# Two of the three weighted one-hot multiplications of the edge preparation issued from GpSimd, and the item's registers loaded inside each step

## The chip, the cores and the metric

One core of a Trainium2 chip runs the whole kernel. The metric is the device time of one execution in microseconds (us). Before the change it is 13,212.99 us, the median of 3 runs.

## What is computed

Four graph layers one after another over 6,250 nodes with 128 features and 200,000 edges sorted by target node; each adds its result to the node features and normalises them.

```python
edge_index = jnp.stack([src, dst])
x = _layernorm(x + _L0_gnn_ref(x, edge_index, edge_weight, ...))       # GCN: segment_sum of h[src] * norm
x = _layernorm(x + _L1_gnn_ref(x, edge_index, edge_type_8, ...))       # gated graph network, 2 rounds, GRU
x = _layernorm(x + _L2_gnn_ref(x, edge_index, ...))                    # graph attention, 8 heads
x = _layernorm(x + _L3_gnn_ref(x, edge_index, edge_attr_64, ...))      # message passing with edge features
# in the GCN: deg = segment_sum(w, dst); norm = deg**-.5[src] * w * deg**-.5[dst]
```

The change lies in a stage that computes no layer by itself. It sorts the edges into records that the layers then read.

## The kernel before

The kernel runs in stages, each a block in which every engine has its own program, with semaphores between the engines. The stage `prep` (its buffers are named `prep_...`) comes third, after the setup of the weights and the making of the work list.

The edges are cut into groups of 1,792 (128 partitions x 14 columns, `GC = 14`). An item is one group seen against one tile of 128 target nodes, 112 items in all; items come from a list in memory, four in each turn of the loop (`SL = 4`), 28 turns. Buffers indexed by `par` are double, by the parity of the item.

For item k the engines do this:

- **SyncE** loads the item's four numbers (base node, column, group, record place) into `itm[:, s]`, two items ahead.
- **GpSimd** (`pool`, lines 687 to 706) loads the group's number into a register, waits until the item two before is through with its buffers, and copies what belongs to the group: L694 and L695 (target and key of each edge), after a wait L698 to L700 (differences to the item's bases), L701, L702 and L704 (the edge's fields: `fld`, two numbers; `w2`, the weight in three bf16 parts, each stored twice; `wm`). The last raises `posted`.
- **VectorE** (`dve`) runs, in one turn of its loop for item k, five functions: `key_hot(k)`, `rank_hot(k-1)`, `rec_add(k-2)`, `weigh_keys(k)`, `window_hot(k)`.
  - `key_hot`: L771 and L772 make the key, L776 the one-hot matrix `OJ` (14 x 98 columns, bf16), which raises `hot_key`; L778, L780 and L781 count equal keys ahead of each edge.
  - `rank_hot`: L795 and L796 take TensorE's counts out of PSUM, L799 and L801 make the rank, L802, L803 the one-hot of the rank, `OHr`; L806 keeps the rank in `RK`.
  - `rec_add`: L816 adds TensorE's placed records to `RECS`, L819 its sums of weights to `acc`.
  - `weigh_keys`: L828, three times: `OJF[..., 2 + a, :] = OJ * w2[a]`, raises `wdone`.
  - `window_hot`: L835 makes the one-hot of the target node, raises `hotd`.
- **ScalarE** scales `OJ` by the two numbers of `fld`: L720, 28 times per item, into `OJF[..., 0:2, :]`, raises `scaled`.
- **TensorE** runs `ranks(k)` (L909 to L914: counts by key), `place(k-1)` (L924: 14 products of `OHr` with all five parts of `OJF`, 490 columns) and `degrees(k)` (L933).

A chain (`Chain.step`, line 91) orders VectorE's dependent steps: each step raises the chain's semaphore at its end, and the engine waits for that count at once, before anything else:

```python
    def step(self, ins):
        ins.then_inc(self.sem, 1)
        self.n += 1
        self.eng.wait_ge(self.sem, self.base + self.n)
```

Addresses that depend on the item come from registers. `places(s)` (lines 784 to 788) increments a semaphore (`passed`) and loads three: the group `g`, the record place `b0` and the column `col`. VectorE calls it once per item ahead of `key_hot` (`now`), which in the order of the program is right behind `window_hot` of the item before, and once more at the start of each turn of the loop (`last`). `rank_hot` and `rec_add` are handed the registers. `w2` and the views `pairs` and `halves` serve the multiplications as pairs of bf16 values.

Of the kernel before, what the change touches and what calls it, by code (L numbers as in the profile page):

```python
# [30 lines left out]
ALU = mybir.AluOpType  # L31
# [80 lines left out]
def build(nc, x, src, dst, edge_attr_64, edge_type_8, edge_weight, L0_gnn_W, L0_gnn_b, L1_gnn_node_proj_w,  # L112
# [47 lines left out]
    with ExitStack() as whole:  # L160
# [442 lines left out]
        with ExitStack() as ctx:  # L603
# [41 lines left out]
            zeroed, posted, hotd, hot_key, scaled, wdone, prefix_ready, prefix_free, hot_rank, place_ready, place_free = sems(  # L645
                "prep", "zeroed posted hotd hot_key scaled wdone prefix_ready prefix_free hot_rank place_ready place_free")
# [5 lines left out]
            with nc.Block() as block:  # L652
# [26 lines left out]
                def _(pool):  # L679
                    pool.wait_ge(zeroed, 1)  # L680
                    n = pool.value_load(turns_to[0:1, NCH:NCH + 1], min_val=1, max_val=KCAP // SL)
                    with pool.Fori(0, n) as i:
                        for s in range(SL):
# [8 lines left out]
                            pool.wait_ge(hotd, k + 1)  # L692
                            fg = FLD[:, ds(g, 1)].rearrange("p g f c -> p (g f) c")
# [11 lines left out]
                            pool.wait_ge(posted, k + 1)  # L705
                            passed(pool, tick)

# [26 lines left out]
                def _(dve):  # L734
# [17 lines left out]
                    dve.sem_inc(scaled, 2)  # L752
                    dve.sem_inc(wdone, 2)
# [12 lines left out]
                    def key_hot(k, s, own):  # L766
# [7 lines left out]
                        dve.wait_ge(scaled, k + 1)  # L774
                        dve.wait_ge(wdone, k + 1)
# [8 lines left out]
                    def places(s):  # L784
                        passed(dve, tick)
                        return (dve.value_load(itm[0:1, s, 2:3], min_val=0, max_val=NG - 1),
                                dve.value_load(itm[0:1, s, 3:4], min_val=0, max_val=(NT - 2) * NT),
                                dve.value_load(itm[0:1, s, 1:2], min_val=0, max_val=N - 1))

                    def rank_hot(k, s, own, at_):  # L790
                        par = s % 2
                        n0 = own.n
                        g, b0, _ = at_
# [16 lines left out]
                    def rec_add(k, s, own, at_):  # L810
                        par = s % 2
                        n0 = own.n
                        _, b0, col = at_
                        dve.wait_ge(place_ready, k + 3)
                        rec = RECS[:, :, ds(b0, BK)]
                        own.step(V.tensor_tensor(out=rec, in0=rec, in1=placed[par].rearrange("p (f b) -> p f b", f=5), op=ALU.add))  # L816
                        dve.sem_inc(place_free, 1)
                        dve.wait_ge(product, k + 3)
                        own.step(V.tensor_tensor(out=acc[0:4, ds(col, P)], in0=acc[0:4, ds(col, P)], in1=dps[par], op=ALU.add))  # L819
                        dve.sem_inc(done, 1)  # L820
                        assert own.n - n0 == ADD_STEPS

                    def weigh_keys(k, s):
# [3 lines left out]
                        for a in range(3):  # L827
                            ins = V.tensor_tensor(out=halves(OJF[:, par, :, 2 + a, :]), in0=halves(OJ[:, par]),  # L828
                                                  in1=pairs(w2[:, par, a], BK), op=ALU.mult)
                        ins.then_inc(wdone, 1)  # L830
# [8 lines left out]
                    with dve.Fori(0, n) as i:  # L839
                        own = Chain(dve, chain)  # L840
                        own.base = i * (SL * STEPS)
                        last = places(SL - 2)
                        for s in range(SL):
                            k = i * SL + s
                            now = places((s - 1) % SL)
                            key_hot(k, s, own)
                            rank_hot(k - 1, (s - 1) % SL, own, now)
                            rec_add(k - 2, (s - 2) % SL, own, last)
                            last = now
# [6 lines left out]
                    last, now = places(SL - 2), places(SL - 1)  # L856
                    rank_hot(n * SL - 1, SL - 1, own, now)
                    rec_add(n * SL - 2, SL - 2, own, last)
                    rec_add(n * SL - 1, SL - 1, own, now)
# [40 lines left out]
                def _(pe):  # L900
# [16 lines left out]
                    def place(k, s):  # L917
                        par = s % 2
                        pe.wait_ge(hot_rank, k + 2)
                        pe.wait_ge(scaled, k + 3)  # L920
                        pe.wait_ge(wdone, k + 3)
# [1405 lines left out]
```

## Time and profile before

| | us |
|---|---|
| median of 3 runs | 13,212.99 |
| the runs | 13,180.84 to 13,275.48 |
| the profiled execution | 13,180.84 |
| its span in the profile | 13,178.7 |
| `prep` loop, first to last item's start | 1,382.6 |

The profile shows one execution. Engines are PE (TensorE matmul), PEld (its weight load), DVE (VectorE), ACT (ScalarE), POOL (GpSimd); a "q" behind a name is the engine's sequencer, whose register and semaphore instructions are not counted as busy. L828 is line 828 of the kernel. Over the whole span PE is busy 47%, DVE 42%, POOL 38%, ACT 12%; these are means over stages with different limits, so the stage's own windows are to be read. "Idle before" names what ended an idle time: another engine's instruction, or "issue" where the profile shows nothing that the engine waited for. The ends of matmuls are modelled.

### The profile page before, as it was taken

The numbers are of one execution on the slowest core, as the hardware profiler recorded it, in microseconds if no ns is written. First come the engines' busy times: TensorE is split into PE (matmuls) and PEld (weight loads), VectorE is DVE, ScalarE is ACT, GpSimd is POOL, SyncE is SP. The second block draws the span as 40 slices with busy tenths as digits, with TensorE's granted clock in tenths as the row PEclk, the third lists the DMA queues.
The fourth block names the chain that finished last, engine by engine and source line by source line (L and its number), as shares of the span: only waits on it lengthen the run. The fifth ranks groups of instructions, "written<-read, shape, count | busy, mean of one in ns | idle before, by whom it ended". The sixth has DMA issues, their size and how long they took to land. (4 is left out here: it accounts for less than half of the span.)

```text
span 13178.7 us, 173973 instructions
## 1 busy us (share of the span) xinstructions
PE 6156.4 (47%) x63984; PEld 5201.2 (39%) x63985; DVE 5472.2 (42%) x6618; ACT 1595.2 (12%) x4258; POOL 5038.6 (38%) x5706
## 2 busy tenths in 40 slices
PE   1666669963233332322222223666996233333344
PEld 1333369951222222212222223556996133333333
DVE  2888878852011111111101114997886312212223
ACT  0666620001000000000000000111000001111111
POOL 0111100002666666566665662000000365565564
PEclk6777789986565666656555555557997566666666
DMA  9000032232112221111111112553221121221121
GB/s 39 0 0 0 0 69 83 83 82 75 45 52 53 55 53 53 50 53 43 43 46 39 42 43 85 207 207 106 94 93 52 46 62 51 54 62 51 52 61 48
DMA packets 572278, 802.99 MB, mean 61 GB/s; under 512 B 400316, under 2 KB 444730, under 8 KB 552872
## 3 DMA queue, kind: packets, MB, share of 16 engines
q1 hardware_dynamic: 397096, 427.95, 12.4%
q0 software_dynamic: 153216, 312.49, 9.4%
q10 hardware_dynamic: 21888, 61.54, 1.2%
q8 instruction: 46, 0.75, 0.0%
q14 instruction: 32, 0.26, 0.0%
HBM read 719.59 MB, written 81.99 MB: 61 GB/s over the span
## 5 line engine op out<-in xcount | busy, mean ns | idle before, releaser
L1088 POOL DMA_INDIRECT ggnn_edges_G<-trans_d,ggnn_edges_idx x3136 | 3117.4, 994 | 2049.5 <-DMA ggnn_edges_idx<-row_d 1102.7
L1196 PE MATMUL ggnn_edges_PS<-ggnn_edges_OH,ggnn_edges_G 128*128 128x128 f32 x6272 | 1081.4, 325 | 2589.1 <-issue 1645.5
L1088 POOL DMA_INDIRECT mpnn_edges_G<-msg_d,mpnn_edges_idx x1568 | 1553.7, 991 | 1398.0 <-DMA mpnn_edges_idx<-src_d 919.1
L1196 PEld LDWEIGHTS ggnn_edges_PS<-ggnn_edges_OH,ggnn_edges_G 128*128 128x128 f32 x6272 | 989.2, 238 | 2687.6 <-issue 2685.8
L1149 DVE TENSOR_TENSOR acc<-acc,ggnn_edges_PS 128x128 f32 x224 | 64.5, 288 | 3034.7 <-remote 2509.9
L720 ACT ACTIVATE prep_OJF<-prep_OJ,prep_fld 128x98 bf16<-128x98 bf16 x3136 | 848.9, 362 | 577.8 <-DVE prep_OJ L776 577.8
L1196 PE MATMUL mpnn_edges_PS<-mpnn_edges_OH,mpnn_edges_G 128*128 128x128 f32 x3136 | 502.3, 307 | 401.1 <-issue 364.0
L924 PE MATMUL prep_PS<-prep_OJF,prep_OHr 128*128 128x490 bf16 x1582 | 582.2, 550 | 226.2 <-DVE prep_OHr L803 226.2
L1174 PE MATMUL mpnn_edges_PS<-wt_late,mpnn_edges_atT 64*128 64x128 f32 x3136 | 351.0, 340 | 667.4 <-ACT mpnn_edges_atT L1064 313.2
L1196 PEld LDWEIGHTS mpnn_edges_PS<-mpnn_edges_OH,mpnn_edges_G 128*128 128x128 f32 x3136 | 450.3, 218 | 456.7 <-issue 452.4
L1376 PE MATMUL heads_GP<-heads_hd,heads_msg 128*128 128x128 f32 x4900 | 590.3, 277 | 0.0
L1376 PE MATMUL gcn_GP<-gcn_hd,gcn_msg 128*128 128x128 f32 x4900 | 590.3, 277 | 0.0
L1174 PEld LDWEIGHTS mpnn_edges_PS<-wt_late,mpnn_edges_atT 64*128 64x128 f32 x3136 | 287.2, 237 | 724.5 <-issue 395.0
L1376 PEld LDWEIGHTS heads_GP<-heads_hd,heads_msg 128*128 128x128 f32 x4900 | 562.8, 192 | 0.1
L1376 PEld LDWEIGHTS gcn_GP<-gcn_hd,gcn_msg 128*128 128x128 f32 x4900 | 562.8, 192 | 0.0
L2027 PE MATMUL ba_XP<-ba_A,ba_hsT 128*128 128x16 bf16 x7350 | 408.4, 174 | 320.2 <-DVE ba_hdT L1911 318.2
L1113 DVE SCALAR_TENSOR_TENSOR ggnn_edges_OH<-dstI,ggnn_edges_itm,iota_row 128x1792 f32<-128x1792 f32 x224 | 464.6, 2084 | 191.7 <-issue 176.5
L1136 DVE TENSOR_TENSOR mpnn_edges_G<-mpnn_edges_G,mpnn_edges_PS 128x896 f32<-128x896 f32 x224 | 233.3, 1082 | 737.1 <-DMA trans_d<-ggnn_edges_tb 610.3
L1536 ACT ACTIVATE ggnn_edges_OH<-ggnn_edges_PS,bcol 128x896 f32<-128x896 f32 x14 | 14.1, 1007 | 4258.0 <-issue 1583.7
L2027 PEld LDWEIGHTS ba_XP<-ba_A,ba_hsT 128*128 128x128 bf16 x7350 | 386.2, 104 | 336.5 <-issue 322.9
L694 POOL COPY prep_dg<-dstI 128x14 int32 x112 | 26.2, 234 | 1191.3 <-PE prep_PS L933 612.9
L1364 PE MATMUL gcn_GP<-gcn_H,gcn_hsT 128*128 128x128 bf16 x7350 | 445.5, 220 | 68.2 <-DVE gcn_hsT L1292 68.2
(462 smaller groups left out, 10687.3 us busy)
## 6 DMA issues: line engine op xcount, KB each, us to landing
ba_rows<-slot_d SPq DMA_DIRECT2D x50, 3136.0 KB
HB<-slot_d SPq DMA_DIRECT2D x50, 1568.0 KB
heads_rows<-slot_d SPq DMA_DIRECT2D x50, 1568.0 KB
ggnn_edges_G<-trans_d,ggnn_edges_idx POOLq DMA_INDIRECT x3136
mpnn_edges_at<-in_edge_attr SPq DMA_DIRECT2D x111, 448.0 KB
trans_d<-gcn_edges_tb ACTq DMA_DIRECT2D x49, 512.0 KB
trans_d<-ggnn_edges_tb ACTq DMA_DIRECT2D x49, 512.0 KB
mpnn_edges_G<-msg_d,mpnn_edges_idx POOLq DMA_INDIRECT x1568
```

The source lines that it names most:

```text
L694: nc.gpsimd.tensor_copy(dg[:], dstI[:, ds(g * GC, GC)])
L720: ins = act.activation(OJF[:, par, c, f, :], OJ[:, par, c, :], ACT.Copy, scale=fld[:, par, f, c:c + 1])
L924: mm = pe.matmul(placed[par], OHr[:, par, c, :], OJF[:, par, c].rearrange("p f b -> p (f b)"), start=c == 0, stop=c == GC - 1)
L1088: pool.indirect_dma_start(G[:, s, c, :], None, table, bass.IndirectOffsetOnAxis(ap=idx[:, s, c:c + 1].bitcast(U32), axis=0)).then_inc(gath ...
L1113: oh = V.scalar_tensor_tensor(out=OH[:, s % 2], in0=over(dst_of[:, ds(g[s] * GC, GC)], P), scalar=itm[:, s, 0:1], in1=rows(iota_row[:], GC ...
L1136: last = V.tensor_tensor(out=ga, in0=ga, in1=ep[a], op=ALU.add)
L1149: V.tensor_tensor(out=acc[:, ds(col, P)], in0=acc[:, ds(col, P)], in1=wp[s % 2], op=ALU.add).then_inc(added, 1)
L1174: mm = pe.matmul(ep[c % 2][:, c // 2, :], atT[h:h + ED, c // 2, :], W(W_M1E)[h:h + ED, :], start=True, stop=True)
L1196: mm = pe.matmul(wp[s % 2], G[:, s, c, :], OH[:, s % 2, c, :], start=c == 0, stop=c == GC - 1)
L1364: mm = pe.matmul(odd if b == 12 else gp[par][:, b], hsT[:, par, b, :], H3[:, a, j * P:(j + 1) * P], start=a == 0, stop=a == 2)
L1376: mm = pe.matmul(accp, msg[:, par, b, :], hd[:, par, b, :], start=j == 0, stop=j == NT - 1)
L2027: pe.matmul(xp[u][:, b], hsT[:, par, b, :], A3[:, first_of[u] + b, a, :], start=a == 0, stop=False, skip_group_check=True)
```

## The change

Three things are done, all in `prep`:

- `weigh_keys` on VectorE keeps only the first of its three multiplications (a = 0). The other two (a = 1, 2) are issued from GpSimd at the end of its item, behind the copies; for them GpSimd waits for `hot_key` (VectorE's L776 of the same item) and `place_ready`. Their second input is `w2[:, par, a, :, 0]`, broadcast over the 98 columns.
- A new semaphore, `pscaled`, is raised by the second of them. `key_hot` on VectorE, `place` on TensorE and the item's start on GpSimd wait for it beside `scaled` and `wdone`.
- `places` is removed. `rank_hot` increments `tick` and loads `g` and `b0` at its own start; `rec_add` does so and loads `b0` and `col` at its start. So there are four loads per item where there were three, and three more per turn of the loop.

```diff
@@ -642,8 +642,8 @@
...
             item_ready = sems("prep", " ".join(f"item_ready{s}" for s in range(SL)))
-            zeroed, posted, hotd, hot_key, scaled, wdone, prefix_ready, prefix_free, hot_rank, place_ready, place_free = sems(
-                "prep", "zeroed posted hotd hot_key scaled wdone prefix_ready prefix_free hot_rank place_ready place_free")
+            zeroed, posted, hotd, hot_key, pscaled, scaled, wdone, prefix_ready, prefix_free, hot_rank, place_ready, place_free = sems(
+                "prep", "zeroed posted hotd hot_key pscaled scaled wdone prefix_ready prefix_free hot_rank place_ready place_free")
             product, done, chain, final, turned, dsq, rooted, tidy, hscaled, stored, listed, filled, copied, cleared, over_ready = sems(
...
@@ -690,6 +690,7 @@
...
                             pool.wait_ge(hotd, k + 1)
+                            pool.wait_ge(pscaled, k + 1)
                             fg = FLD[:, ds(g, 1)].rearrange("p g f c -> p (g f) c")
...
@@ -703,7 +704,13 @@
...
                             pool.wait_ge(posted, k + 1)
+                            pool.wait_ge(hot_key, k + 3)
+                            pool.wait_ge(place_ready, k + 1)
                             passed(pool, tick)
+                            for a in range(1, 3):
+                                ins = nc.gpsimd.tensor_tensor(out=OJF[:, par, :, 2 + a, :], in0=OJ[:, par],
+                                                              in1=over(w2[:, par, a, :, 0], BK), op=ALU.mult)
+                            ins.then_inc(pscaled, 1)
 
...
@@ -750,6 +757,7 @@
...
                     dve.sem_inc(scaled, 2)
+                    dve.sem_inc(pscaled, 2)
                     dve.sem_inc(wdone, 2)
...
@@ -772,6 +780,7 @@
...
                         dve.wait_ge(scaled, k + 1)
+                        dve.wait_ge(pscaled, k + 1)
                         dve.wait_ge(wdone, k + 1)
...
@@ -781,16 +790,12 @@
...
 
-                    def places(s):
-                        passed(dve, tick)
-                        return (dve.value_load(itm[0:1, s, 2:3], min_val=0, max_val=NG - 1),
-                                dve.value_load(itm[0:1, s, 3:4], min_val=0, max_val=(NT - 2) * NT),
-                                dve.value_load(itm[0:1, s, 1:2], min_val=0, max_val=N - 1))
-
-                    def rank_hot(k, s, own, at_):
+                    def rank_hot(k, s, own):
                         par = s % 2
                         n0 = own.n
-                        g, b0, _ = at_
+                        passed(dve, tick)
+                        g = dve.value_load(itm[0:1, s, 2:3], min_val=0, max_val=NG - 1)
+                        b0 = dve.value_load(itm[0:1, s, 3:4], min_val=0, max_val=(NT - 2) * NT)
                         dve.wait_ge(prefix_ready, k + 2)
...
@@ -807,10 +812,12 @@
...
 
-                    def rec_add(k, s, own, at_):
+                    def rec_add(k, s, own):
                         par = s % 2
                         n0 = own.n
-                        _, b0, col = at_
+                        passed(dve, tick)
+                        b0 = dve.value_load(itm[0:1, s, 3:4], min_val=0, max_val=(NT - 2) * NT)
+                        col = dve.value_load(itm[0:1, s, 1:2], min_val=0, max_val=N - 1)
                         dve.wait_ge(place_ready, k + 3)
...
@@ -824,10 +831,8 @@
...
                         dve.wait_ge(place_ready, k + 1)
-                        for a in range(3):
-                            ins = V.tensor_tensor(out=halves(OJF[:, par, :, 2 + a, :]), in0=halves(OJ[:, par]),
-                                                  in1=pairs(w2[:, par, a], BK), op=ALU.mult)
-                        ins.then_inc(wdone, 1)
+                        V.tensor_tensor(out=halves(OJF[:, par, :, 2, :]), in0=halves(OJ[:, par]),
+                                        in1=pairs(w2[:, par, 0], BK), op=ALU.mult).then_inc(wdone, 1)
 
...
@@ -839,24 +844,20 @@
...
                         own.base = i * (SL * STEPS)
-                        last = places(SL - 2)
                         for s in range(SL):
                             k = i * SL + s
-                            now = places((s - 1) % SL)
                             key_hot(k, s, own)
-                            rank_hot(k - 1, (s - 1) % SL, own, now)
-                            rec_add(k - 2, (s - 2) % SL, own, last)
-                            last = now
+                            rank_hot(k - 1, (s - 1) % SL, own)
+                            rec_add(k - 2, (s - 2) % SL, own)
                             weigh_keys(k, s)
...
                     own.base = n * (SL * STEPS)
-                    last, now = places(SL - 2), places(SL - 1)
-                    rank_hot(n * SL - 1, SL - 1, own, now)
-                    rec_add(n * SL - 2, SL - 2, own, last)
-                    rec_add(n * SL - 1, SL - 1, own, now)
+                    rank_hot(n * SL - 1, SL - 1, own)
+                    rec_add(n * SL - 2, SL - 2, own)
+                    rec_add(n * SL - 1, SL - 1, own)
                     dve.sem_inc(final, 1)
...
@@ -918,6 +919,7 @@
...
                         pe.wait_ge(scaled, k + 3)
+                        pe.wait_ge(pscaled, k + 3)
                         pe.wait_ge(wdone, k + 3)
...
```

## Rows read from the trace of the kernel before

**Rows 1.** The page: the span.

```profile
span 13178.7 us, 173973 instructions
```

**Rows 2.** Windows: a turn's last item, the next item, the loop; busy time per engine.

```profile
core 0: us, PE busy (x) PEld busy (x) DVE busy (x) ACT busy (x) POOL busy (x), PEclk, DMA share, GB/s
...
809.30:822.70 13.40, 8.92 (x75) 4.63 (x73) 10.99 (x20) 7.58 (x28) 2.47 (x8) 0.85 0.00 0
822.70:834.84 12.14, 6.65 (x44) 3.39 (x44) 10.88 (x20) 7.58 (x28) 2.60 (x8) 0.72 0.01 0
...
324.00:1706.60 1382.60, 881.25 (x6423) 475.57 (x6424) 1212.21 (x2109) 841.34 (x3108) 250.81 (x888) 0.74 0.01 0
```

**Rows 3.** Groups of instructions, 324 to 1706.6 us: busy, mean ns, idle before.

```profile
L828 DVE TENSOR_TENSOR prep_OJF<-prep_OJ,prep_w 128x1372 bf16<-128x1372 bf16 x333 | 271.0, 870 | 33.3 <-DVE acc L819 33.3
...
L780 DVE TENSOR_TENSOR prep_twin<-prep_twin,prep_lower 128x196 f32<-128x196 f32 x111 | 40.9, 369 | 3.8
...
L771 DVE TENSOR_SCALAR prep_win<-prep_off 128x14 int32<-128x14 int32 x111 | 18.9, 170 | 37.5 <-issue 31.2 <-POOL prep_wm L704 6.3
...
L694 POOL COPY prep_dg<-dstI 128x14 int32 x111 | 26.0, 235 | 1100.0 <-PE prep_PS L933 612.9 <-DVE prep_OJ L776 485.9 <-issue 1.2
```

**Rows 4.** Timeline of VectorE, one item: start us, duration us, instruction, [idle before].

```profile
809.30 0.17 DVE L771 TENSOR_SCALAR prep_win<-prep_off 128x14 int32<-128x14 int32 x1
...
809.73 0.87 DVE L776 TENSOR_TENSOR prep_OJ<-prep_key,prep_iob 128x1372 bf16<-128x1372 bf16 x1
810.52 0.35 DVE L778 TENSOR_TENSOR prep_twin<-prep_key 128x196 f32<-128x196 bf16 x1
810.90 0.36 DVE L780 TENSOR_TENSOR prep_twin<-prep_twin,prep_lower 128x196 f32<-128x196 f32 x1
811.30 0.36 DVE L781 TENSOR_REDUCE prep_within<-prep_twin 128x14 f32<-128x196 f32 x1
...
812.52 0.92 DVE L799 TENSOR_TENSOR prep_prod<-prep_OJ,prep_pfx 128x1372 bf16<-128x1372 bf16 x1 [0.16 <-DVE prep_pfx L796]
...
815.10 0.19 DVE L802 TENSOR_TENSOR prep_rank<-prep_rank,prep_within 128x28 bf16<-128x28 f32 x1
...
818.11 2.44 DVE L828 TENSOR_TENSOR prep_OJF<-prep_OJ,prep_w 128x1372 bf16<-128x1372 bf16 x3 [0.30 <-DVE acc L819]
820.47 1.08 DVE L835 TENSOR_TENSOR prep_OHd<-prep_at,prep_iob 128x1792 bf16<-128x1792 bf16 x1
822.70 0.18 DVE L771 TENSOR_SCALAR prep_win<-prep_off 128x14 int32<-128x14 int32 x1 [1.15 <-issue]
```

**Rows 5.** Lines L786 and L787: ns min/median/max, then first and last start us.

```profile
L786 DVEq TENSOR_LOAD <-prep_itm x142: 299/302/317, 319.4 to 1717.8; - x142
L786 DVEq FUSED_REGOPS  x142: 183/190/190, 319.7 to 1718.1; - x142
...
L787 DVEq TENSOR_LOAD <-prep_itm x142: 297/298/304, 320.0 to 1718.4; - x142
```

**Rows 6.** Timeline of GpSimd, then of VectorE, in the stage before, 218 to 230 us.

```profile
220.35 3.21 POOL L467 TENSOR_TENSOR acc<-wgt,FLD 128x1568 f32<-128x1568 f32 x1
223.62 1.50 POOL L468 CAST FLD<-acc 128x1568 bf16<-128x1568 f32 x1
225.20 2.96 POOL L469 TENSOR_TENSOR acc<-acc,FLD 128x1568 f32<-128x1568 f32 x1
...
220.38 3.32 DVE L490 TENSOR_TENSOR trib<-iota_row,iota_col 128x128 bf16<-128x128 f32 x1
...
225.81 1.79 DVE L494 TENSOR_REDUCE acc<-dstF 128x112 f32<-128x1568 f32 x1
```

**Rows 7.** Timeline of GpSimd in the prep loop, 811 to 826 us.

```profile
812.54 1.04 POOL L700 TENSOR_SCALAR prep_at<-prep_dg,prep_itm 128x28 bf16<-128x28 int32 x1
...
823.50 0.91 POOL L698 TENSOR_SCALAR prep_off<-prep_dg,prep_itm 128x14 int32<-128x14 int32 x1 [0.20 <-POOL prep_kg L695]
...
824.86 0.35 POOL L700 TENSOR_SCALAR prep_at<-prep_dg,prep_itm 128x28 bf16<-128x28 int32 x1
```

**Rows 8.** Timeline of TensorE, then of ScalarE, 803 to 819 us.

```profile
804.29 5.82 PE L924 MATMUL prep_PS<-prep_OJF,prep_OHr 128*128 128x490 bf16 x14 [1.18 <-DVE prep_OHr L803]
...
810.63 7.58 ACT L720 ACTIVATE prep_OJF<-prep_OJ,prep_fld 128x98 bf16<-128x98 bf16 x28 [4.60 <-DVE prep_OJ L776]
```

## Prediction

> **What bounds the kernel now.** I read the page first and then its windows: the change touches one stage, the preparation of the edge list (`prep`). The page [rows 1] gives the span. The windows view [rows 2] gives the stage's loop, which starts at 324 us and whose last item starts at 1706.6 us. In it VectorE (DVE) is busy for 1212.2 of 1382.6 us (88%), ScalarE (ACT) for 61%, TensorE (PE) for 64%, GpSimd (POOL) for 18%. The 111 steps between the first and the last item take 1382.6/111 = 12.46 us each: a step is 12.14 us as from 822.70, or 13.40 us where a new turn of the loop begins at its end, as from 809.30.
>
> Then the timeline of one item on VectorE [rows 4], read as a ring: which gap is there that another engine causes? There is none. From L771 to the next L771 each instruction begins when the one before it ends, apart from steps of its own chain, and the one large gap (1.15 us before L771 at a turn's start) is "issue", the sequencer's own time. The other engines have slack [rows 8]: TensorE's 14 products of L924 start at 804.29 after VectorE's L803 and end at 810.11, half a microsecond before the work of the next item that asks for them (ACT at 810.63); ScalarE's 28 scalings take 7.58 us of the 12.46. GpSimd waits 1100.0/111 = 9.9 us per item before its first copy, L694 [rows 3]. So one item costs what VectorE's instruction stream costs, with its sequencer, and the change is priced as a longer or shorter VectorE ring, times 112 items.
>
> **Part 1: two multiplications leave VectorE.** The L828 group is three instructions in 2.44 us; from its start (818.11) to that of L835 (820.47) are 2.36 us [rows 4], so one costs 0.79 us in the stream (the mean of 870 ns [rows 3] counts the overlap of neighbours twice). Two go: -1.57 us per item.
>
> **Part 2: the register loads move.** This part has nothing to do with GpSimd, and I think that it is the easiest to overlook. `places` reads three registers per item, at the end of an item's stream, while the three L828 multiplications run: L828, L835 and L771 follow each other with no gap in three items of four. Only at a turn's start, where `last` is read too (six loads in a row), does the sequencer come too late: 31.2 us over 27 turns, 0.28 us per item [rows 3]. That goes away, -0.28 us.
>
> In the changed kernel the loads stand inside `rank_hot` and `rec_add`, two in each. Ahead of both stands an `own.step`, whose last act is to wait until the step (L781, and L806) has finished. The sequencer can't run ahead of that wait, so VectorE is empty while the loads run, and the next instruction (L795, L816) needs their registers. A load is a TENSOR_LOAD of 0.30 us, register arithmetic of 0.19 and an assert, and from one load to the next are 0.6 us (L786 first starts at 319.4, L787 at 320.0) [rows 5]. The semaphore increment of `passed` ahead of them costs about what it costs before L799, whose gap is 0.16 us [rows 4]; plain steps follow each other within 0.03. So each place costs 2 x 0.61 + 0.13 = 1.35 us, and both +2.7 us per item. Bounds: if only the TENSOR_LOADs themselves were exposed, 4 x 0.30 = 1.2; if each place had the whole 1.15 us gap of L771 on top of what L835 hides there today, not above 3.2.
>
> Parts 1 and 2 together: 12.46 - 1.57 - 0.28 + 2.7 = 13.31 us. Even if GpSimd's multiplications cost VectorE nothing, the item is 0.85 us longer, 95 us over 112.
>
> **Part 3: what the two multiplications do on GpSimd.** The trace has none of this shape. The nearest are L467 and L469, two-input TENSOR_TENSORs of 128x1568: 3.21 and 2.96 us [rows 6]. Scaled by 1372/1568: 2.8 and 2.6; I take 2.7 us each. The upper bound is 3.2 (the 14 rows of the output lie apart). The lower is the one-input CAST of 1568 elements (1.50 us), scaled: 1.3 us. GpSimd has room: 5.4 + its 2.3 us of copies against 12.46.
>
> But it doesn't run beside VectorE undisturbed. The stage before, which builds the work list, shows it [rows 6]: VectorE's L490, a TENSOR_TENSOR of only 128x128, starts at 220.38, 0.03 us after GpSimd's L467, and takes 3.32 us. It ends 0.15 us after L467 does. VectorE's L494, a reduction with one input, runs through L469 and takes 1.79 us. In the prep loop the reverse is seen [rows 7]: GpSimd's L700, 0.35 us when nothing is in its way, takes 1.04 us when it starts 0.02 us after VectorE's L799, and ends with it. So an instruction of VectorE with two inputs in SBUF and one of GpSimd exclude each other, whole instruction by whole instruction. The Trainium skill states this as a rule ("SBUF — State Buffer", "Who interferes with whom"): VectorE's second SBUF input comes through the read interface that GpSimd uses, whoever starts first has it until its end, and reductions are free of it. By that rule the trace agrees, with the 3.32 us of L490. The skill's "GPSIMD Engine Reference" ("Elementwise — side-by-side cycle accounting") has 4497 ns for a two-input operation of 2048 fp32 elements, which would make an estimate of 3.0 us per multiplication and, put into the sum below, 13,660 us.
>
> Now the place. GpSimd's multiplication waits for `hot_key`, which L776 raises at its end, 1.30 us after L771 (810.60). GpSimd takes 0.20 us over a wait with a semaphore increment (its gap before L698 [rows 7]) and comes to about 1.55. VectorE's L778 ends at 1.57, L780 starts at 1.60. They ask within 0.05 us of each other.
>
> If GpSimd is first: 1.6 to 4.3 us; L780 ends at about 4.5 instead of 1.97, so +2.5. Then the second multiplication, queued, has the interface to 7.2. VectorE meanwhile does what is free of it (L781, two loads, L795, L796), and L799, today at 3.22, would start at 3.22 + 2.5 + 1.35 = 7.1: at most 0.2 us late. Together +2.6 us.
>
> If L780 is first: the multiplication runs 1.95 to 4.65, L799 comes at 4.57. If the second multiplication stands ahead of it, it waits to 7.35: +2.6 again. If L799 goes between the two, the second runs 5.5 to 8.2 and holds L802, due at 7.25: +1.05 in all.
>
> **The sum.** 13.31 + 2.6 = 15.9 us per item, 3.45 us more, times 112 = 386 us. On the profiled execution's 13,180.8 us that makes 13,567. The median of the runs shown, 13,213, lies 32 us above that execution; I take most of it with me: 13,590 us. Nothing else moves: the added waits of VectorE and TensorE on `pscaled` are met long before (the multiplications end 7 us into their item; L924 reads them in the next), and GpSimd's copies for the next item, queued behind them, run from 8 to about 11 us of a 15.9 us item. TensorE's L924 keeps its half microsecond, since it moves with L803.
>
> **Rivals.**
> - *GpSimd and VectorE interleave* (L799 gets in between, or the multiplications are as cheap as a cast, 1.3 us: 1.1 us on L780 and nothing behind). 13.31 + 1.1 = 14.4 us, +1.95 x 112 = 220: 13,430. For it: the order is decided by hundredths of a microsecond.
> - *No blocking, only the loads.* 13.31 us, +95: 13,310. Against it: L490.
> - *Faster: the loads stay hidden*, because the sequencer reads ahead of the chain's wait as it does under L828 today. Then the base is 10.6 us. It is faster than now only if blocking then costs less than 1.85 us per item. With none: -1.85 x 112 = -207, 13,000. With the 2.7 us multiplications held as above, L780 is 2.5 us late and L799, without loads before it, 1.3: 14.4 us, +220 again. So this needs both the hidden loads and an interleave that [rows 6] speaks against.
> - *The multiplications are dearer* than any row (rows of 98 elements, 490 apart): each further 0.5 us is paid about twice on VectorE, +1 us per item, 112 us: 13,700 and above.
>
> **How the numbers follow.** The forecast (13,540 to 13,660 with multiplications of 2.6 to 3.0 us) 0.58; interleaved 0.20; dearer 0.10; only the loads 0.07; faster 0.05. The range 13,390 to 13,780 leaves out the last two and the far end of the dearer ones. About 1% (132 us) is what a measurement here can tell from no change. Faster by over 1%: the loads hidden, 0.04. Within 1%, up to 13,345: only the loads, and some of the mixed cases, 0.09. Slower: 0.87.
>
> **What would show it.** L828 once per item. L795 and L816 with an idle time of about 1.4 us each before them, put down to "issue", and none before L771. L780, 369 ns on the mean now, near 2.9 us (right: GpSimd first), or 369 ns with a long L799 or L802 (interleaved), or none of them long (no blocking). GpSimd's two new TENSOR_TENSORs at 2.7 us. Steps from L771 to L771 of 15.9 us, all four alike. It is wrong if L795 starts right behind L781, or if the L771 steps are under 12.4 us.

## The result and the profile after

The changed kernel takes 13,555.58 us, the median of 4 runs (13,548.45 to 13,621.32), against 13,239.97 us for the kernel before (4 runs, 13,180.84 to 13,275.48): 1.0264 times as long, 95% interval 1.0215 to 1.0312. It is slower, by 316 us between the medians. The profiled execution has a span of 13,565.0 us, 386 us more than that of before [rows 1].

In the changed kernel the lines move: L771 is now L779, L776 is L785, L778 is L787, L780 is L789, L781 is L790, L795 is L800, L799 is L804, L801 and L802 are L806 and L807, L816 is L823, the multiplication left on VectorE (L828) is L834, and GpSimd's two are L711.

The windows view: the setup, the loop of the stage from the first item to the last, and what follows it. In it the loop is 1,727 us long where it was 1,383 us [rows 2].

```profile
core 0: us, PE busy (x) PEld busy (x) DVE busy (x) ACT busy (x) POOL busy (x), PEclk, DMA share, GB/s
0.00:304.00 304.00, 57.93 (x295) 51.04 (x296) 75.76 (x91) 26.08 (x43) 25.04 (x29) 0.69 0.95 43
304.00:2031.00 1727.00, 967.27 (x6422) 555.01 (x6423) 1279.39 (x1887) 841.30 (x3108) 806.02 (x1110) 0.67 0.00 0
```

The loop gives 344 us of the 386 in the span. Setup is 20 us shorter in this execution (the first item starts at 304, not 324 us) and what follows the loop 62 us longer. The change leaves the setup alone and touches only the last three calls behind the loop; the stretch of 83 us right behind the loop is as long as before. The message passing stage alone, which the change doesn't touch, is 64 us longer from its first gathered matmul to its last, and the four runs of before differ by 95 us among themselves.

TensorE has a lower granted clock in this loop, 0.67 where it was 0.74. Both are means over stretches at the upper level (2.4 GHz) and at the lower (1.2): in the item shown below it is 0.90 from 1004 to 1008 us, and 0.50 from 1012 to 1016, behind 5.04 us without a matmul. The matmuls that count keys, of 98 columns, take 284 ns where they took 207 (medians). That costs nothing here: VectorE's waits for TensorE come to 2.4 us in the whole loop (L823 below).

VectorE's timeline over one item of the changed kernel (start us, duration us, instruction, idle before and its releaser), and GpSimd's two multiplications in it:

```profile
1004.17 0.17 DVE L779 TENSOR_SCALAR prep_win<-prep_off 128x14 int32<-128x14 int32 x1
...
1004.63 0.87 DVE L785 TENSOR_TENSOR prep_OJ<-prep_key,prep_iob 128x1372 bf16<-128x1372 bf16 x1
1005.43 0.35 DVE L787 TENSOR_TENSOR prep_twin<-prep_key 128x196 f32<-128x196 bf16 x1
1005.82 2.60 DVE L789 TENSOR_TENSOR prep_twin<-prep_twin,prep_lower 128x196 f32<-128x196 f32 x1
1008.45 0.36 DVE L790 TENSOR_REDUCE prep_within<-prep_twin 128x14 f32<-128x196 f32 x1
1010.29 0.26 DVE L800 TENSOR_SCALAR prep_cnt<-prep_PS 128x98 f32 x1 [1.49 <-issue]
...
1011.00 0.87 DVE L804 TENSOR_TENSOR prep_prod<-prep_OJ,prep_pfx 128x1372 bf16<-128x1372 bf16 x1 [0.15 <-DVE prep_pfx L801]
...
1016.46 0.67 DVE L823 TENSOR_TENSOR X<-X,prep_PS 128x490 f32 x1 [1.53 <-issue]
...
1017.94 0.88 DVE L834 TENSOR_TENSOR prep_OJF<-prep_OJ,prep_w 128x1372 bf16<-128x1372 bf16 x1 [0.29 <-DVE acc L826]
1018.73 1.08 DVE L840 TENSOR_TENSOR prep_OHd<-prep_at,prep_iob 128x1792 bf16<-128x1792 bf16 x1
1019.73 0.17 DVE L779 TENSOR_SCALAR prep_win<-prep_off 128x14 int32<-128x14 int32 x1
```

```profile
1005.72 5.03 POOL L711 TENSOR_TENSOR prep_OJF<-prep_OJ,prep_w 128x1372 bf16<-128x1372 bf16 x2 [8.07 <-DVE prep_OJ L785]
...
1005.72 2.47 POOL L711 TENSOR_TENSOR prep_OJF<-prep_OJ,prep_w 128x1372 bf16<-128x1372 bf16 x1 [8.07 <-DVE prep_OJ L785]
...
1008.15 2.60 POOL L711 TENSOR_TENSOR prep_OJF<-prep_OJ,prep_w 128x1372 bf16<-128x1372 bf16 x1
```

The first line has both multiplications together; the other two, from narrower windows, have each by itself.

Three things differ from [rows 4]. L789 takes 2.60 us where L780 took 0.36: it starts 0.10 us after GpSimd's L711, and ends 0.23 us after GpSimd's first multiplication (1005.72 to 1008.19). L800 and L823 stand behind 1.5 us of "issue" each. And L840 and L779 follow L834 with no gap. GpSimd's second multiplication ends at 1010.75, a quarter of a microsecond before L804 needs two inputs from SBUF: it costs nothing. From L779 to L779 are 15.56 us.

The same in the groups of the loop (busy us, mean ns, idle before and its releasers):

```profile
L711 POOL TENSOR_TENSOR prep_OJF<-prep_OJ,prep_w 128x1372 bf16<-128x1372 bf16 x221 | 556.0, 2537 | 888.2 <-DVE prep_OJ L785 855.9 <-PE prep_PS L926 32.3
L789 DVE TENSOR_TENSOR prep_twin<-prep_twin,prep_lower 128x196 f32<-128x196 f32 x110 | 285.7, 2597 | 3.8
...
L834 DVE TENSOR_TENSOR prep_OJF<-prep_OJ,prep_w 128x1372 bf16<-128x1372 bf16 x111 | 97.0, 874 | 32.6 <-DVE acc L826 32.6
...
L823 DVE TENSOR_TENSOR X<-X,prep_PS 128x490 f32 x113 | 75.3, 667 | 173.2 <-issue 170.8 <-PE prep_PS L926 2.4
...
L800 DVE TENSOR_SCALAR prep_cnt<-prep_PS 128x98 f32 x112 | 29.2, 261 | 165.7 <-issue 165.7
```

L789's mean is 2,597 ns against 369 ns [rows 3]: +2.23 us per item. It is so in every item:

```profile
L789 DVE TENSOR_TENSOR prep_twin<-prep_twin,prep_lower x112: 2595/2597/2602, 305.6 to 2032.8; 128x196 f32<-128x196 f32 x112
```

The idle time before L800 is 165.7/112 = 1.48 us, before L823 170.8/113 = 1.51 us; in the kernel before, the same two gaps were 0.15 us (L781 ends at 811.66, L795 starts at 811.81) and 0.11 us (L806 ends at 816.50, L816 starts at 816.61):

```profile
811.81 0.26 DVE L795 TENSOR_SCALAR prep_cnt<-prep_PS 128x98 f32 x1
...
816.33 0.17 DVE L806 TENSOR_TENSOR prep_RK<-prep_RK,prep_rank 128x14 bf16 x1
816.61 0.67 DVE L816 TENSOR_TENSOR X<-X,prep_PS 128x490 f32 x1
```

That is +1.33 and +1.40. So the item adds up: 12.46 - 1.57 - 0.28 + 2.23 + 1.33 + 1.40 = 15.57 us.

### The profile page after: what moved, and what is told of

Same layout as the page of the kernel before. It is cut to its first block and busy times, and to the rows that moved or that the text cites. A ratio compares the mean times of both kernels' runs of the same rounds, so it can differ in the third digit from the quotient of the medians.

```text
span 13565.0 us, 174256 instructions
## 1 busy us (share of the span) xinstructions
PE 6263.8 (46%) x63984; PEld 5302.1 (39%) x63985; DVE 5538.6 (41%) x6394; ACT 1595.4 (12%) x4258; POOL 5607.3 (41%) x5930
## 5 line engine op out<-in xcount | busy, mean ns | idle before, releaser
L1198 PE MATMUL ggnn_edges_PS<-ggnn_edges_OH,ggnn_edges_G 128*128 128x128 f32 x6272 | 1108.4, 328 | 2726.2 <-issue 1862.5
L1198 PEld LDWEIGHTS ggnn_edges_PS<-ggnn_edges_OH,ggnn_edges_G 128*128 128x128 f32 x6272 | 1009.9, 241 | 2829.6 <-issue 2828.9
L711 POOL TENSOR_TENSOR prep_OJF<-prep_OJ,prep_w 128x1372 bf16<-128x1372 bf16 x224 | 563.5, 2537 | 898.0 <-DVE prep_OJ L785 865.7
L1198 PE MATMUL mpnn_edges_PS<-mpnn_edges_OH,mpnn_edges_G 128*128 128x128 f32 x3136 | 494.9, 308 | 342.0 <-issue 313.6
L926 PE MATMUL prep_PS<-prep_OJF,prep_OHr 128*128 128x490 bf16 x1582 | 586.9, 554 | 140.8 <-DVE prep_OHr L808 140.8
L1198 PEld LDWEIGHTS mpnn_edges_PS<-mpnn_edges_OH,mpnn_edges_G 128*128 128x128 f32 x3136 | 449.5, 220 | 387.8 <-issue 383.2
L1090 POOL DMA_INDIRECT gcn_edges_G<-gcn_d,gcn_edges_idx x28 | 29.8, 1066 | 1122.9 <-DMA gcn_edges_idx<-src_d 1114.7
```

What stands on the lines that cost most here:

```text
L711: ins = nc.gpsimd.tensor_tensor(out=OJF[:, par, :, 2 + a, :], in0=OJ[:, par], in1=over(w2[:, par, a, :, 0], BK), op=ALU.mult)
L926: mm = pe.matmul(placed[par], OHr[:, par, c, :], OJF[:, par, c].rearrange("p f b -> p (f b)"), start=c == 0, stop=c == GC - 1)
L1090: pool.indirect_dma_start(G[:, s, c, :], None, table, bass.IndirectOffsetOnAxis(ap=idx[:, s, c:c + 1].bitcast(U32), axis=0)).then_inc(gath ...
L1198: mm = pe.matmul(wp[s % 2], G[:, s, c, :], OH[:, s % 2, c, :], start=c == 0, stop=c == GC - 1)
```

## The experiments

Ten kernels ran, each compared with runs of the kernel before on the same chip: experiments 1 to 4 on one chip, 5 to 7 on a second, 8 to 10 on a third. There the kernel before takes 11,885 to 11,893 us, and not 13,240 as in the measurement of the result. The prep loop runs at the same pace in both (L801's successor takes 1,582 ns in each); the difference lies in the gathering stages of two later layers. These are the matmuls of the gated graph stage, then of the message passing stage, in the changed kernel as first measured (L1198) and in experiment 1 (L1190); the first and the last start in us stand behind the colon's three durations:

```profile
L1198 PE MATMUL ggnn_edges_PS<-ggnn_edges_OH,ggnn_edges_G x6272: 269/275/578, 3513.2 to 8430.0; 128*128 128x128 f32 x196
...
L1198 PE MATMUL mpnn_edges_PS<-mpnn_edges_OH,mpnn_edges_G x3136: 269/275/580, 10740.5 to 13518.5; 128*128 128x128 f32 x196
```

```profile
L1190 PE MATMUL ggnn_edges_PS<-ggnn_edges_OH,ggnn_edges_G x6272: 274/421/578, 3463.5 to 7686.0; 128*128 128x128 f32 x196
...
L1190 PE MATMUL mpnn_edges_PS<-mpnn_edges_OH,mpnn_edges_G x3136: 273/275/580, 9992.3 to 12113.0; 128*128 128x128 f32 x196
```

4,917 us and 4,223 us for the same work, then 2,778 and 2,121: together 1,351 us, which is all by which the parts behind the loop differ (1,352 us). Why is open: no run separates the chip from anything else that differs between the two measurements. Each measured difference below is between runs on one chip; the items' times are also compared across chips, since the loop has one pace on all. The time per item is from the first item's L771 (or its successor) to the last item's, over 111.

| kernel | item, us | (item - 12.46) x 112 | measured difference | ratio, 95% interval |
|---|---|---|---|---|
| changed kernel | 15.56 | +347 | +316 | 1.0264 (1.0215 to 1.0312) |
| 1 loads only | 14.90 | +273 | +268 | 1.0225 (1.0208 to 1.0242) |
| 2 GpSimd only | 14.48 | +226 | +226 | 1.0190 (1.0173 to 1.0207) |
| 3 nothing on GpSimd | 13.34 | +98 | +91 | 1.0074 (1.0058 to 1.0091) |
| 4 one on GpSimd | 16.36 | +437 | +422 | 1.0354 (1.0337 to 1.0371) |
| 5 GpSimd only writes | 13.33 | +98 | +97 | 1.0082 (1.0065 to 1.0099) |
| 6 one, later | 14.11 | +186 | +176 | 1.0146 (1.0129 to 1.0163) |
| 7 both, later | 14.14 | +188 | +186 | 1.0154 (1.0137 to 1.0171) |
| 8 before, loads under L801 | 12.18 | -31 | -29 | 0.9974 (0.9965 to 0.9984) |
| 9 and one on ScalarE | 11.36 | -123 | -135 | 0.9887 (0.9872 to 0.9902) |
| 10 one on ScalarE | 11.84 | -69 | -70 | 0.9940 (0.9927 to 0.9954) |

The loop alone gives each experiment's difference to within 15 us, and the changed kernel's to within 31 us, in the measurement whose runs scatter more. Nothing outside the loop is needed.

### 1. The loads alone

The kernel before with the change's `rank_hot` and `rec_add`; all three multiplications stay on VectorE.

```diff
-                    def rank_hot(k, s, own, at_):
+                    def rank_hot(k, s, own):
...
-                        g, b0, _ = at_
+                        passed(dve, tick)
+                        g = dve.value_load(itm[0:1, s, 2:3], min_val=0, max_val=NG - 1)
+                        b0 = dve.value_load(itm[0:1, s, 3:4], min_val=0, max_val=(NT - 2) * NT)
```

> The kernel before with only the register loads moved into rank_hot and rec_add (places removed); all three L828 multiplications stay on VectorE and GpSimd gets nothing new. My account (the loads are exposed behind the chain's waits): an idle time of about 1.5 us, put down to issue, ahead of each of the two instructions that need the registers, 1.34 + 1.40 us more than before, the turn's 0.28 us gone: 14.9 us per item instead of 12.46, +275 us. Rival (the loads are free, the whole loss is GpSimd's): 12.2 to 12.5 us per item, no change.

Measured: 14.90 us per item, +268 us. The groups of its loop (L791 is L795 of before, L814 is L816):

```profile
L814 DVE TENSOR_TENSOR X<-X,prep_PS 128x490 f32 x110 | 73.4, 667 | 167.4 <-issue 167.4
...
L791 DVE TENSOR_SCALAR prep_cnt<-prep_PS 128x98 f32 x111 | 29.0, 261 | 166.4 <-issue 166.4
```

1.52 and 1.50 us of idle time per item. Moving the register loads, without touching one vector instruction, costs 85% of what the whole change costs by the medians (268 of 316 us), and 79% by the loop (273 of 347).

### 2. The multiplications alone

The changed kernel with `places` back where it was.

```diff
-                        passed(dve, tick)
-                        g = dve.value_load(itm[0:1, s, 2:3], min_val=0, max_val=NG - 1)
-                        b0 = dve.value_load(itm[0:1, s, 3:4], min_val=0, max_val=(NT - 2) * NT)
+                        g, b0, _ = at_
```

> The changed kernel with the loads put back into places, ahead of key_hot. The two multiplications stay on GpSimd. My account: the step L789 is held as before (+2.23 us); without loads ahead of it the multiplication of the counts (L799 of before) now comes 1.0 us before the second GpSimd multiplication ends and is held too; and the three loads, once hidden under three multiplications of VectorE, stick out under one: 0.7 us in three items of four, 3.0 us at a turn's start, 1.3 us on the mean. 15.1 us per item, +295 us against before, only some 50 us better than the changed kernel. Rival (the loads' place alone decides, undoing it gives it all back): 12.8 us per item, +40 us. Rival (both multiplications are fully paid whatever stands around them): over 16 us.

Measured: 14.48 us per item, +226 us, between my 15.1 and the first rival's 12.8, nearer to mine. The groups of its loop (L808 is L799 of before, L779 is L771):

```profile
L789 DVE TENSOR_TENSOR prep_twin<-prep_twin,prep_lower 128x196 f32<-128x196 f32 x111 | 225.7, 2033 | 3.8
L808 DVE TENSOR_TENSOR prep_prod<-prep_OJ,prep_pfx 128x1372 bf16<-128x1372 bf16 x111 | 216.1, 1947 | 17.6 <-DVE prep_pfx L805 17.5
L811 DVE TENSOR_TENSOR prep_rank<-prep_rank,prep_within 128x28 bf16<-128x28 f32 x111 | 41.3, 372 | 3.8
L779 DVE TENSOR_SCALAR prep_win<-prep_off 128x14 int32<-128x14 int32 x111 | 19.4, 175 | 100.6 <-issue 94.2 <-POOL prep_wm L705 6.4
```

The second multiplication, free in the changed kernel, now holds L808: 1,947 ns where L799 took 900, so +1.05 us, as I expected. The loads stick out as expected in kind, 94.2/111 = 0.85 us per item, though I had 1.3. L789 is held by 1.66 us on the mean, not 2.23.

The trace shows why. GpSimd's wait ends with TensorE's place (L932), not with `hot_key`, in 28 of the 112 items; its multiplication starts later in them, and VectorE's L789 has gone first. One such item, of GpSimd and then of VectorE:

```profile
1033.69 5.54 POOL L711 TENSOR_TENSOR prep_OJF<-prep_OJ,prep_w 128x1372 bf16<-128x1372 bf16 x2 [7.57 <-PE prep_PS L932]
```

```profile
1032.89 0.36 DVE L789 TENSOR_TENSOR prep_twin<-prep_twin,prep_lower 128x196 f32<-128x196 f32 x1
...
1034.49 2.40 DVE L808 TENSOR_TENSOR prep_prod<-prep_OJ,prep_pfx 128x1372 bf16<-128x1372 bf16 x1 [0.16 <-DVE prep_pfx L805]
...
1038.55 0.73 DVE L811 TENSOR_TENSOR prep_rank<-prep_rank,prep_within 128x28 bf16<-128x28 f32 x1
```

L789 takes 0.36 us in each of the 28 items, the first multiplication holds L808 (2.32 us on the mean), L808 gets in ahead of the second, and the second holds L811 (0.73 us). In the other 84 items they take 2.60, 1.81 and 0.25. So in a quarter of the items the order of the interleaved rival came about by itself, and such an item is the shorter one (13.01 us from L779 to L779, where its neighbour without a turn's start takes 14.13).

The two halves of the change, +268 and +226, add up to far more than its +316. In the whole, the loads inside `rank_hot` give the second multiplication a place in which it hides, and no loads stick out at the item's end, as they do here.

### 3. Nothing on GpSimd

The changed kernel; the two lower bf16 parts of the weight are not multiplied.

```diff
-                            for a in range(1, 3):
-                                ins = nc.gpsimd.tensor_tensor(out=OJF[:, par, :, 2 + a, :], in0=OJ[:, par],
-                                                              in1=over(w2[:, par, a, :, 0], BK), op=ALU.mult)
-                            ins.then_inc(pscaled, 1)
+                            nc.gpsimd.sem_inc(pscaled, 1)
```

> The changed kernel without the two GpSimd multiplications: GpSimd only raises the semaphore, parts 1 and 2 of the weight stay zero, so the two lower bf16 parts of the weights are left out of the computation. My account: L789 falls from 2.6 to 0.37 us and nothing else changes, 15.56 - 2.23 = 13.33 us per item, +98 us against before: taking two of VectorE's instructions away with their whole work still loses to the kernel before. Rival (the loads take the place of waits that come back): 12.5 us or less.

Measured: 13.34 us per item, +91 us. VectorE has two instructions less per item and nobody does their work, and the kernel is still slower than before. Against the changed kernel the item is 2.22 us shorter, what L789 loses.

### 4. One multiplication back on VectorE

```diff
-                            for a in range(1, 3):
+                            for a in range(2, 3):
```

> The changed kernel with one multiplication on GpSimd and two on VectorE. My account: the first GpSimd multiplication is the one that holds L789, the second runs under L790 and the loads and costs nothing, so taking it back to VectorE saves nothing there and costs its 0.79 us: 15.56 + 0.79 = 16.35 us per item, +436 us against before, slower than the changed kernel. Rival (each of the two costs VectorE half of the 2.23 us): 15.24 us, +312 us.

Measured: 16.36 us per item, +422 us, slower than the changed kernel. L789 takes 2,602 to 2,608 ns in every item. Half of the work on GpSimd has the full price. It isn't the amount of GpSimd's work that VectorE pays; it pays for what GpSimd is doing at the moment at which L789 comes.

### 5. GpSimd only writes

```diff
+                            nc.gpsimd.memset(OJF[:, par, :, 3:5, :], 0.0).then_inc(pscaled, 1)
```

in place of both multiplications.

> The changed kernel with one GpSimd memset of the same 14 x 196 bf16 elements in place of the two multiplications, at the same point and about as long as one of them (estimate 2.3 us, from the memset of 5120 elements in 4.35 us); the two lower parts of the weights are left out of the computation. It only writes. My account (VectorE's second input and GpSimd's input share one way into SBUF): a memset asks for no input, L789 stays at 0.37 us, 13.33 us per item as without anything on GpSimd, +95 us against before. Rival (any GpSimd instruction of that length holds VectorE off): L789 about 2.3 us, 15.3 us per item, +315 us.

Measured: 13.33 us per item, +97 us. The memset is as long as a multiplication and starts as close ahead of the same instruction of VectorE (L786 here; both timelines over one item):

```profile
1004.14 2.38 POOL L710 MEMSET prep_OJF<- 128x2744 bf16 x1 [8.34 <-DVE prep_OJ L782]
```

```profile
1004.27 0.36 DVE L786 TENSOR_TENSOR prep_twin<-prep_twin,prep_lower 128x196 f32<-128x196 f32 x1
```

L786 runs through in 0.36 us. So what excludes the two engines here is GpSimd's reading. On VectorE's side, the instructions with one input that lie beside the second multiplication in the changed kernel (L790, L800 and L801) have their usual 0.36 and 0.26 us; only instructions with two inputs from SBUF are held. That is how the Trainium skill has it ("SBUF — State Buffer", "Who interferes with whom"): a two-input instruction of VectorE contends with a GpSimd instruction that reads SBUF, not with one that only writes it. This pair of runs agrees, 2.60 us against 0.36.

### 6. One multiplication, later

Experiment 4 with one wait more on GpSimd: it starts when L789 (L790 here) has ended. `STEPS` is 13 steps per item, L789 is the fourth.

```diff
+                            pool.wait_ge(chain, k * STEPS + 4)
                             for a in range(2, 3):
```

> The run with one multiplication on GpSimd and two on VectorE (16.36 us per item), with one wait more: GpSimd starts only when L789 has ended. From there VectorE needs 2.6 us (L790, the two loads, L800, L801) until it next reads two inputs from SBUF, and the multiplication takes 2.54. My account: the same instructions cost VectorE nothing there, L789 0.37 us, L804 at most 0.3 us late: 13.33 + 0.79 = 14.1 to 14.4 us per item, +190 to +220 us against before. Rival (the two engines slow each other by their amount of work, not by whom starts first): about 16.3 us, +430 us.

Measured: 14.11 us per item, +176 us, against 16.36 and +422. An additional wait on the slower engine takes 2.25 us off the item. GpSimd's multiplication, then VectorE's L790 and L805 (the L799 of before):

```profile
1004.76 2.48 POOL L712 TENSOR_TENSOR prep_OJF<-prep_OJ,prep_w 128x1372 bf16<-128x1372 bf16 x1 [8.97 <-DVE prep_twin L790]
```

```profile
1004.31 0.36 DVE L790 TENSOR_TENSOR prep_twin<-prep_twin,prep_lower 128x196 f32<-128x196 f32 x1
...
1007.27 0.88 DVE L805 TENSOR_TENSOR prep_prod<-prep_OJ,prep_pfx 128x1372 bf16<-128x1372 bf16 x1 [0.15 <-DVE prep_pfx L802]
```

The multiplication lies between two instructions that need the same way into SBUF, and both have their usual length.

### 7. Both multiplications, later

The changed kernel, the first after L789, the second after L804.

```diff
                             for a in range(1, 3):
+                                pool.wait_ge(chain, k * STEPS + (4 if a == 1 else 8))
```

> The changed kernel, both multiplications on GpSimd, with two waits more: the first starts when L789 has ended, the second when L804 has. My account: the first hides as in the run before it; the second runs under L806 (1.58 us, one input) and holds L807 by about 1.0 us: 13.33 + 1.0 + 0.1 = 14.4 us per item (15.56 in the changed kernel), +220 us against before. Rival (amount of work decides): 15.6 us, +350 us.

Measured: 14.14 us per item, +186 us. The second multiplication (1005.60, 2.48 us) holds L808 (0.19 us when free), as expected, by 0.76 us:

```profile
1005.60 2.48 POOL L712 TENSOR_TENSOR prep_OJF<-prep_OJ,prep_w 128x1372 bf16<-128x1372 bf16 x1 [0.98 <-DVE prep_prod L805]
```

```profile
1005.56 1.58 DVE L807 TENSOR_REDUCE prep_rank<-prep_prod 128x14 f32<-128x1372 bf16 x1
1007.17 0.95 DVE L808 TENSOR_TENSOR prep_rank<-prep_rank,prep_within 128x28 bf16<-128x28 f32 x1
```

The reduction L807, with one input, is not touched. The first multiplication is hidden, the second costs 0.76 us, and the kernel still loses 1.68 us per item to the kernel before. Without the 0.76 it would still lose 0.9 (an estimate): that much is the loads.

### 8. The loads where they cost nothing

The kernel before. At a turn's start it reads six registers in a row; the three for `last` are now two (`b0` and `col`) that stand behind the issue of the reduction L801 and ahead of the wait for it.

```diff
-                        own.step(V.tensor_reduce(rank[:], prod[:], AX, ALU.add))
+                        red = V.tensor_reduce(rank[:], prod[:], AX, ALU.add)
+                        red.then_inc(own.sem, 1)
+                        own.n += 1
+                        rec_at = places2(s_rec) if s_rec is not None else None
+                        own.eng.wait_ge(own.sem, own.base + own.n)
```

> The kernel before, with one thing moved: at a turn's start the registers for rec_add are loaded behind the issue of the reduction L801 (1.58 us) and ahead of the wait for it, two loads of 0.61 us, instead of a third round of places in a row. My account: the 1.15 us gap at a turn's start goes, all four items take 12.15 us: -0.3 us per item, -34 us (0.3%). Rival (the loads delay the step that waits for the reduction): no change.

Measured: 12.18 us per item, -29 us (0.9974, interval 0.9965 to 0.9984). Two loads that cost 1.3 to 1.4 us in front of a step cost nothing behind one that is running, here once in four items: L771, which stood behind 31.2 us of "issue" [rows 3], has none:

```profile
L771 DVE TENSOR_SCALAR prep_win<-prep_off 128x14 int32<-128x14 int32 x109 | 18.2, 167 | 0.0
```

### 9 and 10. The multiplication on ScalarE

The goal of the change, less work for VectorE, with an engine that had 5 us free per item [rows 2]: ScalarE scales `OJ` by a third field, and GpSimd has one small copy more for it.

```diff
-            fld = sb(ctx, "prep_fld", [P, 2, 2, GC])
+            fld = sb(ctx, "prep_fld", [P, 2, 3, GC])
...
+                            nc.gpsimd.tensor_copy(fld[:, par, 2], fg[:, 4, :])
...
-                                for f in range(2):
-                                    ins = act.activation(OJF[:, par, c, f, :], OJ[:, par, c, :], ACT.Copy,
+                                for f in range(3):
+                                    ins = act.activation(OJF[:, par, c, (0, 1, 4)[f], :], OJ[:, par, c, :], ACT.Copy,
...
-                        for a in range(3):
+                        for a in range(2):
```

> As the run before it, and one of the three weight multiplications of VectorE goes to ScalarE, as a third field of its scalings (42 instead of 28 per item, 0.27 us each: 11.4 us per item where it had 7.6); GpSimd has one more small copy. ScalarE shares no way into SBUF with VectorE in any row so far. My account: VectorE's item falls to 12.14 - 0.79 = 11.35, ScalarE's 11.4 becomes about the bound: 11.5 us per item, -107 us (0.8%), faster than both kernels. Rival (ScalarE becomes the bound with its waits): over 12 us, less than half of it. Rival (ScalarE's reads slow VectorE as GpSimd's do): slower than before.

> ScalarE's third field alone, the loads as in the kernel before. Three items of four 11.45 us; at a turn's start the six loads set the time, which one multiplication fewer does not shorten, 13.4 us: 11.95 us per item, -57 us (0.45%).

Measured: with the loads of experiment 8, 11.36 us per item and -135 us (0.9887, interval 0.9872 to 0.9902); alone, 11.84 us and -70 us. ScalarE's row over the loop of experiment 9:

```profile
L721 ACT ACTIVATE prep_OJF<-prep_OJ,prep_fld 128x98 bf16<-128x98 bf16 x4650 | 1247.3, 362 | 10.6 <-PE prep_PS L935 9.2 <-DVE prep_OJ L777 0.6
```

It is busy for 1,247 us and idle for 10.6. So ScalarE is now about as full as VectorE, and a second multiplication would not fit: 56 scalings at the 0.27 us that one takes in [rows 8] (7.58/28) would be 15 us per item, an estimate. Experiment 9 beats the kernel before by 135 us, where the changed kernel loses 316 to it.

## Why the prediction was right, point by point

- **The bound.** The item was VectorE's stream with its sequencer, and it stayed so. TensorE's place stays short of the bound (L926 ends 32.3 us of GpSimd's 888 us of waiting, in 4 of 112 items, and 2.4 us of VectorE's).
- **Two multiplications fewer, -1.57 us.** L828's successor L834 stands once per item. Experiment 4, which puts one back, is 16.36 - 15.56 = 0.80 us longer; the step had 0.79.
- **The turn's gap, -0.28 us.** Gone: L840 and L779 follow each other.
- **The loads, +2.7 us.** Measured +2.73, and alone in experiment 1, 14.90 - 12.46 + 0.28 = 2.72. The rival in which the sequencer reads ahead fell there.
- **GpSimd's multiplication, 2.7 us.** It takes 2.54 on the mean: 2.47 the first, 2.60 the second, and 2.48 where nothing is near it (experiment 6). The rows scaled by the element count gave 2.6 and 2.8, from fp32 inputs; the estimate of 3.0 us worked out from the Trainium skill's "GPSIMD Engine Reference" ("Elementwise — side-by-side cycle accounting") is too high here.
- **The hold, +2.5 us on L780 and 0.1 behind it.** Measured +2.23 and nothing. This is the term that was too large. I had the multiplication at 1.6 to 4.3 us into the item and the end of L780 0.2 us behind, at 4.5. It runs from 1.55 to 4.02, and L789 ends at 4.25: nearly all of the difference is the shorter multiplication (2.47 for 2.7).
- **The order, GpSimd first.** The forecast did not decide it: it took +2.6 us for two of the three orders and left the third to a rival. The two starts are 0.10 us apart, GpSimd first in all 112 items, and where the order turns, as in 28 items of experiment 2, the interleaved rival's order appears and the item is shorter. That it did not turn in the changed kernel is in part luck. One of the sums was wrong besides: with L780 first and the second multiplication ahead of L799, the wait to 7.35 from 4.57 is 2.8 us, not 2.6; that case didn't occur.
- **The faster rival.** In its sum with the multiplications held, L799 would be 1.5 us late and not 1.3 (7.2 against 3.22 + 2.5). Experiment 2 comes nearest to it: the loads are not behind the chain's waits there, but they don't stay hidden either (0.85 us at the item's end), and L799's successor is held by 1.05 us on the mean.
- **The sum.** 15.9 us predicted per item, 15.56 measured; 386 us against 347 from the loop and 316 between the medians. The forecast of 13,590 us lies 34 us above the median of 13,556, closer than its parts allow: runs of one kernel lie up to 95 us apart here. The difference that it stood for, 377 us on 13,213, is 61 us above the 316 measured; 27 us of that are made up by the kernel before, whose median came out at 13,240.
- **The interleaved rival** (L799 between the two multiplications) didn't happen in the changed kernel. Experiment 7 brings the order about by its waits, and the second multiplication holds L802's successor by 0.76 us where the rival had 0.95; experiment 2 has it in 28 items, with 0.54 us on that instruction but 1.4 us on L799's successor, which comes 1.35 us earlier there, without the loads in front of it.

## What to carry to other kernels

Here a register load costs nothing while its engine works on something already issued (experiment 8), and its full 0.6 us behind a wait for that engine's own last step (experiment 1); moving loads "to where they are used" moved them behind such waits. Work that is handed from VectorE to GpSimd is not hidden because GpSimd is idle: an instruction of VectorE with two inputs from SBUF that starts while a GpSimd multiplication reads SBUF waits for its end (L789, 2.60 us for 0.37), so long GpSimd instructions belong into stretches in which VectorE reduces, reads one input from PSUM or waits, and an added wait can be what puts them there (experiment 6). Where another engine is free that holds up no instruction of VectorE, as ScalarE in experiment 9 (L781 stays at 0.36 us), take that one.

## What the runs showed of the hardware that I had not expected

Two engines' instructions, 0.10 us apart at their starts, decide over 2.23 us, and they do so in the same order in all 112 items of the changed kernel: L789 takes 2,595 to 2,602 ns. With the loads moved back, the same code has the other order in 28 items (experiment 2). A GpSimd wait more made a kernel 246 us faster (experiments 4 and 6). And the same work of the two gathering stages took 1,351 us less in one measurement than in another, so that only differences taken on one chip could be compared; the cause of that is open.
